# A two-stage convolution kernel: squares of the inner image move from ScalarE to GpSimd, one more tap on VectorE in even halves

## The reference, cut to what matters

```python
pooled = x.mean((2, 3))
hdn = _ln(pooled @ w_fc1.T, ln1_w, ln1_b, axis=-1)
dyn_w = (hdn @ w_fc2.T).reshape(b * c, 1, K, K)          # a 5x5 kernel for each image and channel
out = depthwise_conv(x, dyn_w, padding=2)
u = out.mean(1, keepdims=True)
s2 = jnp.square(out - u).mean(1, keepdims=True)
out = ln2_w * (out - u) * lax.rsqrt(s2 + EPS) + ln2_b     # over the channels, for each pixel
out = gelu(einsum('bchw,oc->bohw', out, w_expand))       # 64 -> 256 channels
gx = jnp.sqrt(jnp.sum(jnp.square(out), axis=(2, 3), keepdims=True))
out = gamma * (out * gx / (gx.mean(1, keepdims=True) + EPS)) + beta + out
return einsum('bohw,co->bchw', out, w_shrink) + x
```

## Time and profile before

| | |
|---|---|
| median of 3 runs | 834.87 us (834.35 to 836.52) |
| profiled execution, its own time | 837.79 us |
| its span | 836.1 us |
| TensorE busy | 777.7 us (93%) |
| VectorE busy | 620.9 us (74%) |
| ScalarE busy | 405.0 us (48%) |
| GpSimd busy | 461.2 us (55%) |
| TensorE's mean granted clock | 0.979 |

### The profile page before, as it was taken

One profiled execution on the slowest core, in us unless ns is written; L12 is line 12 of the kernel. 1 busy time (PEld: TensorE's weight loads), 2 busy tenths in 40 slices (PEclk: granted clock), 3 DMA queues, 4 the chain that ended last, 5 costly groups with the idle time before them and its releaser, 6 DMA issues. The chain is left out here.

```text
span 836.1 us, 15638 instructions
## 1 busy us (share of the span) xinstructions
PE 777.7 (93%) x5399; PEld 639.0 (76%) x5399; DVE 620.9 (74%) x1138; ACT 405.0 (48%) x496; POOL 461.2 (55%) x455
## 2 busy tenths in 40 slices
PE   5999999999999999999999997778899999999876
PEld 5999998999998999999999996544444445454332
DVE  3666666666666666667888888988999898989965
ACT  5591002777773000000000005458989999999981
POOL 2333333333332333335888883985879898898610
PEclk9999999999999999999999997978999999999999
DMA  6770000000000000000000002132233334433234
GB/s 145 159 176 0 0 0 1 1 0 0 0 0 1 1 0 0 0 0 2 0 0 0 0 0 50 34 72 66 65 79 79 81 100 107 103 78 79 57 76 101
DMA packets 61571, 35.81 MB, mean 43 GB/s; under 512 B 41504, under 2 KB 59488, under 8 KB 61536
## 3 DMA queue, kind: packets, MB, share of 16 engines
q1 hardware_dynamic: 59424, 34.83, 17.7%
q10 hardware_dynamic: 2112, 0.52, 0.3%
HBM read 17.85 MB, written 9.37 MB: 33 GB/s over the span
## 5 line engine op out<-in xcount | busy, mean ns | idle before, releaser
L504 PE MATMUL psum<-line_hi,taps_hi 128*128 128x256 f32 x1270 | 203.0, 292 | 11.8 <-DVE taps_lo L400 8.6
L518 PE MATMUL psum<-line_lo,taps_hi 128*128 128x256 f32 x1270 | 202.6, 291 | 0.8 <-DVE line_lo L453 0.8
L512 PE MATMUL psum<-line_hi,taps_lo 128*128 128x256 f32 x1270 | 202.5, 291 | 0.0
L453 DVE SCALAR_TENSOR_TENSOR line_lo<-psum,rest 128x256 fp32r<-128x256 f32 x254 | 108.1, 425 | 124.3 <-POOL rest L285 114.3
L504 PEld LDWEIGHTS psum<-line_hi,taps_hi 128*128 128x128 f32 x1270 | 177.1, 192 | 13.0 <-issue 9.3
L518 PEld LDWEIGHTS psum<-line_lo,taps_hi 128*128 128x128 f32 x1270 | 176.7, 192 | 1.9 <-DVE line_lo L453 1.7
L512 PEld LDWEIGHTS psum<-line_hi,taps_lo 128*128 128x128 f32 x1270 | 177.1, 192 | 0.0
L285 POOL TENSOR_TENSOR rest<-x,line_hi 128x256 f32<-128x256 f32 x127 | 82.9, 653 | 169.0 <-DVE line_hi L444 169.0
L793 POOL TENSOR_TENSOR part<-part,prod 128x945 f32<-128x945 f32 (+2 forms) x61 | 138.5, 2271 | 17.8 <-ACT prod L860 11.3
L285 POOL TENSOR_TENSOR rest<-by_h,line_hi 128x256 f32<-128x256 f32 x127 | 91.6, 721 | 83.4 <-DVE line_hi L444 83.4
L337 ACT ACTIVATE by_h<-x (+1 forms) x128 | 85.7, 669 | 107.0 <-DVE x L433 105.4
(11 more groups left out here) (159 smaller groups left out, 767.7 us busy)
## 6 DMA issues: line engine op xcount, KB each, us to landing
stage<-in_x_dram SPq DMA_DIRECT2D x32, 256.0 KB, 4.0
rstd_wide<-rstd_dram SPq DMA_DIRECT2D x30, 256.0 KB, 5.3
out_dram<-x SPq DMA_DIRECT2D x28, 256.0 KB, 5.5
crossed<-x SPq DMA_DIRECT2D x16, 256.0 KB, 3.5
crossed<-x SPq DMA_DIRECT2D x16, 240.0 KB, 3.3
rstd_dram<-rstd SPq DMA_DIRECT2D x15, 64.0 KB, 1.5
out_dram<-x ACTq DMA_DIRECT2D x4, 128.0 KB, 4.8
out_dram<-x SPq DMA_DIRECT2D x4, 128.0 KB, 4.2
```

The costliest lines, as they stand in the source:

```text
L453: dve.scalar_tensor_tensor(out=line_lo[:, (slot + 1) % SLOTS, :, part], in0=as_lines(line_ps[slot][:, 0:LINE]), scalar=0.0, in1=as_lines(r ...
L504: mm = pe.matmul(line_ps[slot][:, 0:LINE], taps_hi[:, s, d, :], line_hi[:, slot, :, d:d + WP], start=(d == 0), stop=(d == OFFSETS - 1))
L512: pe.matmul(line_ps[slot][:, 0:LINE], taps_lo[:, s, d, :], line_hi[:, slot, :, d:d + WP], start=False, stop=False, skip_group_check=True)
L518: mm = pe.matmul(line_ps[slot][:, 0:LINE], taps_hi[:, s, d, :], line_lo[:, slot, :, d:d + WP], start=False, stop=(d == OFFSETS - 1), skip_ ...
```

## The change

ScalarE's `square` is taken out of its slot loop and from the steps after the loop. GpSimd gets a `square` of its own, a `tensor_tensor` multiply of the image with itself, with the same waits. It stands first in each of GpSimd's slots, ahead of `norm`, and after the loop behind `norm(LAST - 1)`. `EARLY` gains the halves 6, 8, 10, 12 and 14: VectorE takes eleven taps there, ScalarE makes four products and GpSimd three adds. In the halves of `EARLY`, the slot takes one more tap ahead of the response steps.

```diff
-EARLY, EARLY_TAP = (3, 4, 5,), ("up", 3)
+EARLY, EARLY_TAP = (3, 4, 5, 6, 8, 10, 12, 14,), ("up", 3)
...
 (GpSimd)
+            def square(u):
+                pool.wait_ge(tap_step, taps_end(u))
+                if u > 0:
+                    pool.wait_ge(stats_done, u)
+                image = inner[:, u % INNERS, :, :].rearrange("p j w -> p (j w)")
+                pool.tensor_tensor(squares[:, :], image, image, ALU.mult).then_inc(squared, 1)
...
             for s in range(UNITS):
                 e = s - 2
+                if s >= 1:
+                    square(s - 1)
                 if e >= 0:
                     norm(e)
...
             make_spread()
             norm(LAST - 1)
+            square(LAST)
...
 (ScalarE)
-            def square(u):
-                act.wait_ge(tap_step, taps_end(u))
-                if u > 0:
-                    act.wait_ge(stats_done, u)
-                act.activation(squares[:, :], inner[:, u % INNERS, :, :].rearrange("p j w -> p (j w)"),
-                               ACT.Square).then_inc(squared, 1)
...
-                if w in range(UNITS):
-                    square(w)
                 if n in range(UNITS):
                     add_squares(n, 1)
...
             add_squares(LAST - 2, 1)
-            square(LAST)
             act.activation(hid_stat[:, 0:1], eps_col[0:B, :], ACT.Sqrt)
...
 (VectorE)
                     finish(v, 1)
-                take(1)
+                take(1 + len(dve_taps(s)) - len(DVE_TAPS))
                 if n in range(UNITS) and n % 2 == 1:
                     respond(n // 2)
```

## The result

The changed kernel takes 838.39 us (median of 12 runs, 836.73 to 839.79); the kernel before takes 835.25 us in the same session (12 runs, 834.35 to 836.71). The ratio is 1.003, with a 95% interval of 1.0022 to 1.0039: slower by 3.1 us. The change costs something between 0 and 3 us, and two of the three places where I looked for it are right. One of the 12 executions of the first experiment was slow, 855.14 us at a mean granted clock of 0.84, and is left out of its ratio.

The account below looks back on a forecast made before the run. The prediction took TensorE's path with one exposed gelu to bound the 18.0 us slots. Terms of -0.4 + 1.4 + 3.0 = +4.0 us turned the median 834.87 into 838.9 us, range 836.2 to 841.4.

Parts of the forecast that it names:

- Which wait ends last: Steady slots: TensorE's 16.79 us plus one exposed gelu with hand-overs make 18.0 us; removing ScalarE's square there gains nothing.
- Start, -0.4 us: Slots 3 and 4: without ScalarE's square, mean_sq starts 0.22 us earlier each time, -0.4 us in all.
- VectorE's tap, 0: Five slots: the new 1.25 us tap fills VectorE's 1.24 us wait for the response mean, cost 0.
- Stall of expand (0,0), +1.4 us: Slots 7, 9, 11, 13: GpSimd's square delays norm, so TensorE stalls 0.34 us each, +1.4 us.
- a square under 2 us: Sign that the forecast is wrong: GpSimd squares were expected at 2.3 to 2.4 us.
- Every two-input row is dearer than the cast: Argument against pricing GpSimd's square as one input at 1.04 us, a rival with chance 0.07.
- my bounds: Price limits for GpSimd's square: 1.04 us, a one-input cast, and 2.88 us, a 256-column subtraction times four.
- x_lo's 2.01 us: Rival: GpSimd's square costs 2.01 us like x_lo; no stall, +2.6 us at the end, 837.1 us; chance 0.08.
- End, +3.0 us: After the loop: the last square queues behind norm of half 14, ends 3.21 us later, 0.22 us slack, +3.0 us.
- The sum: Whole kernel: -0.4 + 1.4 + 3.0 = +4.0 us, 838.9 us on the median.
- a fall after the gap at 804 us: TensorE's granted clock falling after the longer gap near the end; about 1 us more, inside the range.
- The clock rival: Slots 2 to 4: earlier work keeps TensorE's clock up from 0.72, 3.2 us less, 835.7 us; chance 0.05.

Follow-up runs that it names:

- the first experiment: The changed kernel with the square of half 15 given back to ScalarE: 835.83 us, ratio 0.9997 to the kernel before.
- the re-ordering: Convolution piece conv(4) moved ahead of expand (1,0), tried on four kernels, with squares on GpSimd or ScalarE: 830.43, 827.09, 826.63 and 827.02 us.
- taps and products alone: The kernel before with only the new taps and products, all squares staying on ScalarE: 835.90 us, ratio 0.9995.
- the priced forms: The changed kernel with ten more two-input GpSimd operations of 128x1024 after its last square, to price them: 844.27 us in one run.
- the second's: A second session timing the unaltered changed kernel again beside the kernel before: 837.05 us against 836.38 us, ratio 1.0009.

## Why the prediction was right, and where it was not

**Which wait ends last: right.** I said that ScalarE's 17.37 us busy of 18 were not the limit and that TensorE's path with one exposed gelu was. Taking squares off ScalarE left the slot at 17.99 us in every kernel without the re-ordering; filling TensorE's wait shortened it in all four with it, to 17.53 to 17.66 us. Both are shown.

**Start, -0.4 us: right at like clock.** The two intervals shrank by 0.22 and 0.19 us. At a higher clock GpSimd's lateness appears (1.72 and 0.45 us), which the kernel before did not show and I did not price.

**VectorE's tap, 0: right.** It fills the 1.24 us wait; taps and products alone give 0.9995.

**Stall of expand (0,0), +1.4 us: wrong, it is 0.** The mis-sized term is the square: 1.86 us to the next start and not 2.34, together with a wake of 0.08 and not 0.18 us. That is 0.48 + 0.10 us, and turns a stall of 0.34 into a margin of 0.24; 0.27 was measured. Of the signs that I had named for being wrong, "a square under 2 us" came. "Every two-input row is dearer than the cast" was right, but the row that I chose reads two tensors and the square reads one. The price lies between my bounds and nearest to x_lo's 2.01 us, whose rival, without a stall and with 837.1 us, had the better mechanism and only 0.08 of the chances. That x_lo's result type would explain its price is not borne out: the type changes nothing in the priced forms. What makes x_lo 2.01 us is open.

**End, +3.0 us: right in mechanism, +2.34 us in size.** The square stands behind the norm, which stands behind its DMA. The last square takes 1.89 us and not 2.38, which is 0.49 us of the 0.66 between the two; crossed starts 0.66 us after inner's start here and 0.80 us after it in the earlier trace rows, which is 0.14; and the square starts 2.31 us after crossed and not 2.34, the last 0.03.

**The sum.** With what was measured it is -0.4 + 0 + 2.34 = +1.9 us, against +4.0 predicted; on 834.87 us that makes 836.8 and not 838.9. Between the two profiled executions of like clock the spans differ by +1.3 us, of which -0.45 us lie in the last piece, which has no change in it. The first session's +3.1 us, nearest to my number, and the second's +0.7 us lie on either side. That 838.4 us lies next to 838.9 is therefore in part luck: what put the first session 1.6 us above 836.8 is not the stall of 1.4 us that I had put there, for it never came. What made the two sessions differ by 2.4 us is open; the clock of slots 2 to 5 is a candidate, as the start piece differs by 3.3 us between executions whose code there is the same, but no run shows it for the timed executions.

**TensorE's clock.** I looked for a fall after the gap at 804 us. It came ahead of that, in slot 15, and is covered in the changed kernel; where the cover is gone it costs 1.1 us. The clock rival's 3.2 us was worked out from counts of instructions that do not carry it: with the same code in that stretch, the kernel with taps alone shows 15.81 us busy as before, but x102 and not x73, at 0.91. That the start piece of these two executions differs by 97.63 - 94.36 = 3.3 us agrees by chance.

## What to carry to other kernels

An engine that is busy 96% of a stretch need not bound it: ask for whom the others wait, and fill that wait before you move work. Price an operation by a row with the same number of distinct inputs, and when a margin is smaller than the spread of possible prices (here a stall of 0.34 us, with prices for the square from 2.01 to 2.88 us), forecast both cases. Cut the spans of two executions at common operations before you compare them: here the whole spans had the wrong sign.

## What the runs showed of the hardware

A GpSimd product of 128x1024 f32 takes 1.89 us if both inputs are the same tensor, and 2.36 us if they are two; the result's type makes no difference. The Trainium skill's rule of the prediction ("GPSIMD Engine Reference", 3.1) covers two inputs, and its estimate of 2.22 us is nearer to the second; no run here says what the chip does with one address given twice beyond its price.

GpSimd and VectorE blocked each other by whole instructions in the one place where VectorE's reduction, with both inputs in SBUF, met GpSimd's operations: 1.23 became 3.15 us, and a group of two GpSimd operations took 8.18 us, where the dearest clean ones take 2 x 2.37. In the steady slots of the changed kernel nothing of this shows; the inner add, with one input in SBUF and one in PSUM, takes 1.22 us beside a nearly full GpSimd, as before.

TensorE's granted clock, 1.00 in slot 15 of the kernel before, is 0.91 or 0.92 there in every kernel of the old order in which GpSimd makes the square of half 14, and where the last shrink group of eight matmuls met the fall it took 3.61 us and not 1.94. TensorE's waits in that slot are as long in sum in both, 5.26 and 5.38 us; they stand in other places. No run here separates what decides.
